# Four-stage cross attention on one core: where the norms' statistics stand, which engine takes the inverse root, and the listed order

## The chip, the cores and the metric

The kernel runs on one core of one Trainium2 chip, as one launch. The time is the device time in microseconds of that core. Lower is better. Engines: TensorE (PE in the profile, PEld its weight loads), VectorE (DVE), ScalarE (ACT), GpSimd (POOL) and SyncE (SP), which issues the DMAs.

## The reference

The input x is 16 batches of 128 rows by 256 columns in float32, ctx has the same shape. Four attention stages follow one another. In the excerpt below the names and masks are shortened.

```python
# stage 0: attention over the 256 columns of x, per batch, with ctx as keys and values
q, k, v = x^T Wq + bq, Wk^T ctx + bk, Wv^T ctx + bv
x = v softmax(q k)^T + x
# stage 1: 16 heads of 16; LN is (x - mean) * rsqrt(var + 1e-5) * scale + bias over the 256 columns
x = x + attention(LN1(x) @ w_qkv + b_qkv, causal mask) @ w_ao + b_ao
x = x + attention(LN2(x) @ w_q, ctx @ w_kv, cross mask) @ w_co + b_co
x = x + gelu(LN3(x) @ w1 + b1) @ w2 + b2
# stage 2: x are the latents; keys and values from ctx and x together
a = attention(x @ q_w, [ctx, x] @ kv_w, mask) @ out_w + out_b + x
x = gelu(RMS(a) * w @ mlp_w1 + b1) @ mlp_w2 + b2 + x
# stage 3: 16 heads of 128, one learned key and value more
x = x + attention(LNA(x) @ wq1, ctx @ wk1, ctx @ wv1) @ wo1 + bo1
x = x + attention(LNB(x) @ wq2, ctx @ wk2, ctx @ wv2) @ wo2 + bo2
x = x + gelu(LNM(x) @ w_fc1 + b_fc1) @ w_fc2 + b_fc2
```

There are thus four norms per batch in stages 1 and 2 (ln1, ln2, ln3 and rms) and three in stage 3.

## The kernel before

All of x lives in SBUF, in the tile X, for the whole kernel. Stages 0 to 2 are one block of code (`stages_0_to_2`), stage 3 is another (`stage_3`). In the block of stages 0 to 2 a group is two batches (NA = 2), so there are eight groups, 0 to 7. Work on several groups is interleaved. A name such as ln2/3 is norm ln2 of group 3. "chan" is stage 0's attention, "self" and "cross" are those of stage 1, "lat" that of stage 2, and mlp1 and mlp2 the two multilayer parts.

Each engine runs a list of pieces written out by hand: TENSOR_ORDER, VECTOR_ORDER, SCALAR_ORDER, GPSIMD_ORDER and LOAD_ORDER (for the DMA queue). A list is given as a string of letters, the *_STEPS, which says from which stream the next piece is taken. Engines work strictly in the order of their own list, and wait for each other through semaphores that are derived from the places in these lists.

A unit of attention goes through these pieces: "scores" (TensorE, L1118 and L1122, and L1110 for chan), "front" on VectorE (mask and row maximum, L801, L808, L779), "exps" (ScalarE, L640), "rsum" on VectorE (the reciprocal of the sum, L817), "normalise" on GpSimd (L590), "turn" on TensorE (transposition of the probabilities, L1135), a copy of it by ScalarE (L648) or VectorE (L823), and "values" on TensorE (L1155, L1165, L1168). After that come the output projection and the residual on VectorE (L839, or L828 for chan), which is followed by the statistics of its rows (bn_stats, L831 and L847).

A norm in stages 0 to 2 is one piece of VectorE. It waits for the xhat of the norm before, aggregates the statistics of the two batches (L859), adds epsilon (L867, for rms L863 and L865), makes the inverse root from an integer guess (L879, L881) and three Newton steps of three instructions each (L885, L887, L889), and then writes xhat (L873, L875). Each small instruction waits for the one before. TensorE transposes xhat (L984), ScalarE scales it on its way out of PSUM (L679, L681), and the projections read that. The statistics of ln1 lie in one buffer of two batches, `stats["ln1"]`, which every group's channel residual writes. A buffer with a place for each of the 16 batches, `row_stats`, holds the statistics of stage 2's result for stage 3's first norm.

GpSimd has, beside the normalises, the additions of bias rows to X (L571, L563), the masks (L577, L584) and, near the end, the low halves of split operands.

Stage 3 has two attention layers of eight pairs of heads. Their matmuls take operands split into a high and a low part, three passes each. GpSimd makes the low parts (L1522 for weights, L1532 for the normed rows, L1537 and L1543 for the last weights, L1549). A norm's factors come from `norm_factors` on VectorE for a slice of batches: aggregation (L1336), variance (L1338), guess (L1340, L1342), Newton steps (L1346, L1348, L1350) and the shift, minus mean times root (L1353). The even rows of xhat are then written by VectorE (L1855) and the odd ones by ScalarE (L1632), which waits for the shift. There are five calls: the first 12 batches while stages 0 to 2 run out, batches 12 to 15 at the opening of stage 3, all 16 at the turn between the two layers, and 0 to 7 and 8 to 15 at the end. At the end the last weights are split beside the norm.

Of the kernel before, what the change touches and what calls it, by code (L numbers as in the profile page):

```python
# [111 lines left out]
def steps_of(step, items):  # L112
# [14 lines left out]
    lat/0 self_q/2 self_k/2 cross_v/1 lat_k/0 lat_q/0 chan_v/3 self_v/2 ctx_v/0 chan_q/3 ctx_k/0 lat_v/0  # L127
    cross_k/2 chan_k/3 cross_o/1 self_o/2 ln3/1 mlp1_up1/1 ln2/2 mlp1_up0/1 cross_q/2 mlp1_up3/1 mlp1_up2/1
    mlp1_down0/1 mlp1_down1/1 ln1/3 lat/1 self_q/3 self_k/3 cross_v/2 lat_k/1 lat_q/1 lat_o/0 chan_v/4
    self_v/3 ctx_v/1 chan_q/4 ctx_k/1 lat_v/1 cross_k/3 chan_k/4 rms/0 cross_o/2 mlp2_up1/0 mlp2_up0/0  # L130
    mlp2_up2/0 mlp2_up3/0 self_o/3 ln3/2 mlp2_down0/0 mlp2_down1/0 mlp1_up1/2 ln2/3 mlp1_up0/2 cross_q/3
    mlp1_up3/2 mlp1_up2/2 mlp1_down0/2 mlp1_down1/2 ln1/4 lat/2 self_q/4 self_k/4 cross_v/3 lat_k/2 lat_q/2
    lat_o/1 chan_v/5 self_v/4 ctx_v/2 chan_q/5 ctx_k/2 lat_v/2 cross_k/4 chan_k/5 rms/1 cross_o/3 mlp2_up1/1
    mlp2_up0/1 mlp2_up2/1 mlp2_up3/1 self_o/4 ln3/3 mlp2_down0/1 mlp2_down1/1 mlp1_up1/3 ln2/4 mlp1_up0/3
    cross_q/4 mlp1_up3/3 mlp1_up2/3 mlp1_down0/3 mlp1_down1/3 ln1/5 lat/3 self_q/5 self_k/5 cross_v/4 lat_k/3
    lat_q/3 lat_o/2 chan_v/6 self_v/5 ctx_v/3 chan_q/6 ctx_k/3 lat_v/3 cross_k/5 chan_k/6 rms/2 cross_o/4
    mlp2_up1/2 mlp2_up0/2 mlp2_up2/2 mlp2_up3/2 self_o/5 ln3/4 mlp2_down0/2 mlp2_down1/2 mlp1_up1/4 ln2/5
# [122 lines left out]
def stages_0_to_2(nc, dram, consts, early):  # L260
# [8 lines left out]
    with ExitStack() as ctx:  # L269
# [207 lines left out]
        with nc.Block() as block:  # L477
# [280 lines left out]
            def _(dve):  # L758
# [90 lines left out]
                def norm(name, g):  # L849
# [1461 lines left out]
```

## Time and profile before

| | |
|---|---|
| runs | 2037.19, 2037.76, 2043.94 us; median 2037.76 |
| the profiled execution | 2035.49 us, its span 2033.5 |
| TensorE busy | 1916.0 us, 94% |
| VectorE busy | 1250.8 us, 62% |
| ScalarE busy | 1186.0 us, 58% |
| GpSimd busy | 676.1 us, 33% |
| stages 0 to 2 | up to about 880 us of the span |

The page's chain of waits puts half of the span on TensorE, most of it on stage 3's projections. Busy shares over the whole span hide the stages. From 100 to 880 us VectorE and ScalarE are busy around 80% beside TensorE; in stage 3 they are near half. The profile is of one execution, and times within it are counted from the start of its span.

### The profile page before, as it was taken

How to read it: one execution, taken by the hardware profiler on the slowest of the kernel's cores; microseconds unless marked ns; L12 is line 12 of the kernel's file. 1: busy time of each engine (PE TensorE's matmuls, PEld its weight loads, DVE VectorE, ACT ScalarE, POOL GpSimd, SP SyncE). 2: the span in 40 equal slices, each digit the busy share in tenths (PEclk: the TensorE clock that was granted, in tenths of full speed). 3: DMA queues.
4: the chain of work that ended last, by engine and by line, in shares of the span. 5: the costliest groups of instructions: out<-in, count | busy, mean ns of one | idle time of the engine just before them, and what ended most of it. 6: DMA issues, size and time to landing. Idle time of an engine off the chain costs nothing.

```text
span 2033.5 us, 43191 instructions
## 1 busy us (share of the span) xinstructions
PE 1916.0 (94%) x14880; PEld 1672.4 (82%) x14880; DVE 1250.8 (62%) x4143; ACT 1186.0 (58%) x3879; POOL 676.1 (33%) x613
## 2 busy tenths in 40 slices
PE   5689999999999999989999999999999999999888
PEld 3467878787878777778999999998899999999778
DVE  3678887887878774644555555556455555555753
ACT  3577888887888876654444444444544444444531
POOL 2334444444444434522221222232321222213452
PEclk7899999999999999999999999999999999999999
DMA  7000000000000000010000000000000000000100
GB/s 271 9 12 9 5 10 5 9 7 1 7 1 4 2 2 23 1 35 27 27 21 15 26 15 26 21 16 17 27 22 16 26 15 26 21 10 0 42 11 32
DMA packets 24635, 44.35 MB, mean 22 GB/s; under 512 B 2336, under 2 KB 12064, under 8 KB 23584
## 3 DMA queue, kind: packets, MB, share of 16 engines
q1 hardware_dynamic: 24336, 42.19, 6.4%
q8 instruction: 85, 1.39, 0.3%
q14 instruction: 70, 0.57, 0.1%
q10 hardware_dynamic: 144, 0.20, 0.0%
HBM read 40.28 MB, written 2.10 MB: 21 GB/s over the span
## 4 chain that ended last, share of the span: by engine, by line
PE 50%; DVE 2%; ACT 2%; issue 1%; POOL 1%; ACTq 0%; DVEq 0%; POOLq 0%
PE general L1988 33%; PE o_psum L2045 6%; PE scores L2027 5%; PE pT_psum L2104 3%; PE scores L2154 1%; ACT probs L1659 1%; POOL probs L1563 1%; PE o_psum L2154 1%; PE pT_psum L2154 1%; PE general L1999 0%; DVE oT L1830 0%; ACT oT L1675 0%; DVE guess L1340 0%; DVE var L1338 0%; DVE row_stats L1792 0%
## 5 line engine op out<-in xcount | busy, mean ns | idle before, releaser
L590 POOL TENSOR_TENSOR probs<-probs,rsums 128x512 f32<-128x512 f32 (+1 forms) x288 | 282.0, 994 | 429.6 <-DVE rsums L817 429.1
L1563 POOL TENSOR_TENSOR probs<-probs,rsums 128x512 f32<-128x512 f32 x128 | 133.3, 1041 | 733.1 <-DVE rsums L1823 733.1
L640 ACT ACTIVATE probs<-negated,negmax 128x128 f32<-128x128 f32 (+1 forms) x768 | 325.6, 429 | 32.8 <-DVE negmax L808 26.0
L1667 ACT COPY probsT<-pT_psum 128x512 f32<-128x512 f32 x128 | 75.0, 586 | 282.6 <-PE pT_psum L2104 282.6
L1988 PE MATMUL general<-hT,w_qk 128*128 128x512 f32 x768 | 206.3, 404 | 1.8 <-ACT kT L1642 1.5
L1135 PE MATMUL pT_psum<-ident,probs 128*128 128x128 f32 x1072 | 171.6, 280 | 33.7 <-ACT probsT L648 20.4
L1988 PE MATMUL general<-w_o,oT 128*128 128x256 f32 x1536 | 197.3, 281 | 1.6 <-ACT oT L1675 0.9
L1988 PE MATMUL general<-ctxT,w_qk 128*128 128x512 f32 x750 | 195.4, 396 | 2.9 <-DVEq L245 2.9
L1988 PEld LDWEIGHTS general<-w_o,oT 128*128 128x128 f32 x1536 | 187.4, 188 | 11.6 <-DVE oT L1830 4.0
L1675 ACT ACTIVATE oT<-o_psum,hcols 128x512 fp32r<-128x512 f32 x128 | 88.1, 689 | 183.8 <-PE o_psum L2045 183.8
L1659 ACT ACTIVATE probs<-scores,negmax 128x128 f32<-128x128 f32 x512 | 180.5, 370 | 24.0 <-DVE negmax L1815 24.0
L1135 PEld LDWEIGHTS pT_psum<-ident,probs 128*128 128x128 f32 x1072 | 123.7, 141 | 85.3 <-ACT probsT L648 38.4
L1988 PEld LDWEIGHTS general<-w_v,ctxT 128*128 128x128 f32 x1488 | 179.9, 189 | 4.6
L1988 PE MATMUL general<-w_v,ctxT 128*128 128x256 f32 x1488 | 181.9, 279 | 0.0
L1830 DVE SCALAR_TENSOR_TENSOR oT<-o_psum,hcols,oT 128x512 fp32r<-128x512 f32 x128 | 96.0, 750 | 119.5 <-ACT oT L1675 119.5
L1988 PEld LDWEIGHTS general<-ctxT,w_qk 128*128 128x128 f32 x750 | 140.1, 189 | 32.9 <-DVEq L245 3.3
L1988 PEld LDWEIGHTS general<-hT,w_qk 128*128 128x128 f32 x768 | 136.2, 189 | 26.5 <-issue 2.1
L997 PE MATMUL general<-hT_y,weights_a 128*128 128x256 f32 x640 | 152.1, 382 | 3.3 <-ACT upT L713 1.2
L640 ACT ACTIVATION_READ_ACCUMULATOR probs<-negated,negmax 128x1 f32 x768 | 147.3, 192 | 0.0
L2045 PE MATMUL o_psum<-probsT,ctxT 128*128 128x128 f32 x1024 | 141.5, 281 | 1.4 <-ACT probsT L1667 1.4
L823 DVE COPY probsT<-pT_psum 128x512 f32<-128x512 f32 (+1 forms) x140 | 91.2, 652 | 83.3 <-PE pT_psum L1135 82.1
L1812 DVE TENSOR_REDUCE rawmax<-scores 128x4 f32<-128x512 f32 x128 | 88.3, 690 | 83.8 <-PE scores L2027 83.8
(199 smaller groups left out, 3869.6 us busy)
## 6 DMA issues: line engine op xcount, KB each, us to landing
raw_qk<-w_qk_dram SPq DMA_DIRECT2D x32, 256.0 KB, 2.8
weights_a<-weights_a_dram SPq DMA_DIRECT2D x2, 2048.0 KB, 18.7
raw_v<-w_v_dram SPq DMA_DIRECT2D x16, 256.0 KB, 2.7
raw_vrows<-vrows_dram SPq DMA_DIRECT2D x16, 256.0 KB, 3.4
raw_o<-w_o_dram SPq DMA_DIRECT2D x16, 256.0 KB, 2.7
weights_a<-weights_a_dram SPq DMA_DIRECT2D x3, 1024.0 KB, 11.7
ctx_in<-ctx_dram SPq DMA_DIRECT2D x8, 256.0 KB, 2.9
X<-x_dram SPq DMA_DIRECT2D x8, 256.0 KB, 16.1
```

The lines of the kernel that those rows point to most:

```text
L590: nc.gpsimd.tensor_tensor(pr, pr, rsums[:, n % 4, 0:segs].unsqueeze(2).broadcast_to([P, segs, width(kind) // segs]), ALU.mult).then_inc(s[ ...
L640: last = nc.scalar.activation(probs[:, n % PROBS, i * wide:(i + 1) * wide], src[:, i * wide:(i + 1) * wide], ACT.Exp, scale=1.0 if kind == ...
L823: nc.vector.tensor_copy(probsT[:, n % 4, 0:width(kind)], turned(kind, g, u)[:, 0:width(kind)]).then_inc(s["pT_copied_dve"], 1)
L997: last = nc.tensor.matmul(out[:, j * RA:(j + 1) * RA], w[weight][:, c, chunk * P:(chunk + 1) * P], rhs(c), start=(c == 0), stop=(c == KC - 1))
L1135: last = nc.tensor.transpose(turned(kind, g, u)[:, j * P:(j + 1) * P], probs[:, n % PROBS, j * P:(j + 1) * P], ident[:, :])
L1563: nc.gpsimd.tensor_tensor(pr, pr, rsums[:, t % 2, :].unsqueeze(2).broadcast_to([P, NB, P]), ALU.mult).then_inc(s["probs_ready"], 1)
L1659: nc.scalar.activation(probs[:, t % 2, b * P:(b + 1) * P], scores[t % 2][:, b * P:(b + 1) * P], ACT.Exp, bias=negmax[:, t % 2, b:b + 1], s ...
L1812: nc.vector.tensor_reduce(rawmax[:, t % 2, :], scores[t % 2][:, :].rearrange("p (b k) -> p b k", b=NB), axis=AX.X, op=ALU.max, negate=True ...
L1830: nc.vector.scalar_tensor_tensor(out=oT[:, LO, head, quarter(t % G)], in0=o_psum[:, :], scalar=hcols[:, bass.ds(at, 1)], in1=oT[:, HI, hea ...
L1988: last = nc.tensor.matmul(out, stationary(a, c), moving(b, c), start=(i == 0), stop=(i == len(terms) - 1))
L2027: last = nc.tensor.matmul(scores[t % 2][:, j * P:(j + 1) * P], qT[:, head, b * P:(b + 1) * P], kT[:, head, b * P:(b + 1) * P], start=True, ...
L2045: last = nc.tensor.matmul(o_psum[:, j * P:(j + 1) * P], v[:, head, (t % G) * NB + j, :], probsT[:, j * P:(j + 1) * P], start=True, stop=True)
```

## The change

- The statistics of ln1 go into `row_stats`, at the place of each batch, in place of `stats["ln1"]`.
- The inverse root is one instruction of GpSimd: a power with exponent -0.5 from a constant tile `halves`, filled by a memset at the start. The guess and the Newton steps are gone, in stages 0 to 2 and in stage 3.
- A norm of stages 0 to 2 is now two pieces of VectorE, "norm" up to the variance and "xhat" behind it, with "root" on GpSimd between them. VectorE's list may have other pieces between the two. In stage 3 the five calls are split in the same way into `variances`, `inverse_roots` and `shifts`. The one for the first 12 batches is moved ahead in VectorE's list; its variance comes before the last group's units and its shift among them.
- The lists of all five queues are new. The strings differ in many places; the start of two of them is shown.

The lists, decoded: on GpSimd the two cross masks, which stood between the third and the fourth normalise of chan/0, stand behind the third normalise of self/0, and the mask of lat/0 moves from place 15 to place 5. On VectorE the pieces between norm and xhat number 0 in nine of the 32 norms, 1 in seven and up to 9 in the others. 408 lines of the decoded lists of TensorE differ between the two in a line by line comparison.

```diff
@@ -121,30 +121,30 @@
 WORK_ORDER = listed("""
-    chan_v/0 chan_q/0 chan_k/0 ln1/0 self_q/0 self_k/0 chan_v/1 self_v/0 chan_q/1 cross_k/0 chan_k/1 self_o/0
-    ln2/0 cross_q/0 ln1/1 self_q/1 self_k/1 cross_v/0 chan_v/2 self_v/1 chan_q/2 cross_k/1 chan_k/2 cross_o/0
+    chan_v/0 chan_q/0 chan_k/0 ln1/0 self_q/0 self_k/0 chan_v/1 chan_q/1 self_v/0 cross_k/0 chan_k/1 self_o/0
+    ln2/0 cross_q/0 ln1/1 self_q/1 chan_v/2 self_k/1 cross_v/0 self_v/1 chan_q/2 chan_k/2 cross_k/1 cross_o/0
...
 LOAD_WORDS = listed("""
-    ctx/2 ctx/3 mask_lat/1 mask_cross/2 ctx/4 mask_lat/2 mask_cross/3 ctx/5 mask_lat/3 mask_cross/4 ctx/6
-    mask_lat/4 mask_cross/5 ctx/7 mask_lat/5 mask_cross/6 mask_lat/6 mask_cross/7 mask_lat/7
+    mask_lat/1 ctx/2 mask_cross/2 ctx/3 mask_lat/2 ctx/4 mask_cross/3 mask_lat/3 ctx/5 mask_cross/4
+    mask_cross/5 ctx/6 mask_lat/4 mask_cross/6 mask_cross/7 mask_lat/5 ctx/7 mask_lat/6 mask_lat/7
...
 GPSIMD_STEPS = (
-    "pppxxpppppppappyppppappapppyppppxppppppppapp...
+    "ppppmyapppxxpyppppppmppmapappppppppppppppppm...
...
-                      w=steps_of("read", [...]), n=steps_of("norm", NORM_ORDER),
+                      w=steps_of("read", [...]), n=steps_of("norm", NORM_ORDER), q=steps_of("xhat", NORM_ORDER),
...
-                      k=..., z=[("first_norm", "x", GA - 1, 0)])
+                      k=..., z=[("first_norm", "x", GA - 1, 0)], i=[("first_shift", "x", GA - 1, 0)])
...
+GPSIMD_ORDER = merged(GPSIMD_STEPS, ..., m=steps_of("root", NORM_ORDER), ..., j=[("first_root", "x", GA - 1, 0)])
...
-        stats = {name: sb("stats_" + name, [P, NA, 6]) for name in NORMS}
+        stats = {name: sb("stats_" + name, [P, NA, 6]) for name in ("ln2", "ln3", "rms")}
...
+                nc.gpsimd.memset(consts["halves"][:, :], -0.5).then_inc(consts["halves_ready"], 1)
...
+                def root(name, g):
+                    pool.wait_ge(s["var_ready"], NORM_ORDER.index((name, g)) + 1)
+                    nc.gpsimd.tensor_tensor(rstd[:, :], var[:, :], consts["halves"][:, 0:NA], ALU.pow).then_inc(s["root_ready"], 1)
...
-                    step(nc.vector.bn_stats(stats["ln1"][:, b, :], x))
+                    step(nc.vector.bn_stats(consts["row_stats"][:, NA * g + b, :], x))
...
-                        step(nc.vector.bn_aggr(mv[:, b, :], stats[name][:, b, :]))
+                        step(nc.vector.bn_aggr(mv[:, b, :], consts["row_stats"][:, NA * g + b, :] if name == "ln1" else stats[name][:, b, :]))
...
-                        step(nc.vector.tensor_scalar(var[:, :], mv[:, :, 1], 1e-5, None, ALU.add))
-                    wait_step()
-                    inverse_root()
+                        nc.vector.tensor_scalar(var[:, :], mv[:, :, 1], 1e-5, None, ALU.add).then_inc(s["var_ready"], 1)
+
+                def xhat_of_rows(name, g):
+
+                    src = Xl[:, :, :] if name == "rms" else X[:, batches(g), :]
+                    dve.wait_ge(s["root_ready"], NORM_ORDER.index((name, g)) + 1)
+                    dve.sem_inc(s["wait_passed"], 1)
...
-                def inverse_root():
-                    step(nc.vector.tensor_single_scalar(guess[:, :], var[:, :].bitcast(I32), 1, ALU.logical_shift_right))
-                    wait_step()
-                    step(nc.vector.tensor_scalar(guess[:, :], guess[:, :], -1.0, RSQRT_MAGIC, ALU.mult, ALU.add))
-                    wait_step()
-                    y = guess[:, :].bitcast(F32)
-                    for i in range(NEWTON_STEPS):
...
+def variances(dve, early, stats, bs):
+    nc = early["nc"]
+    mv, var = early["mv"], early["var"]
+    for b in range(bs.start, bs.stop):
+        early["steps"][0] += 1
+        nc.vector.bn_aggr(mv[:, b, :], stats[:, b, :]).then_inc(early["s"]["norm_step"], 1)
+    dve.wait_ge(early["s"]["norm_step"], early["steps"][0])
+    nc.vector.tensor_scalar(var[:, bs], mv[:, bs, 1], 1e-5, None, ALU.add).then_inc(early["s"]["factors_var"], 1)
+
+def inverse_roots(pool, early, consts, bs, call):
+    pool.wait_ge(early["s"]["factors_var"], call)
+    early["nc"].gpsimd.tensor_tensor(early["rstd"][:, bs], early["var"][:, bs], consts["halves"][:, bs], ALU.pow).then_inc(early["s"]["factors_root"], 1)
+
+def shifts(dve, early, bs, call):
+    dve.wait_ge(early["s"]["factors_root"], call)
+    early["nc"].vector.scalar_tensor_tensor(out=early["shift"][:, bs], in0=early["mv"][:, bs, 0], scalar=-1.0, in1=early["rstd"][:, bs],
+                                            op0=ALU.mult, op1=ALU.mult).then_inc(early["s"]["norm_ready"], 1)
...
                         if kind == "end":
+                            if t == STEPS - 1:
+                                inverse_roots(pool, early, consts, slice(0, B // 2), 4)
...
                     if kind == "turn":
+                        inverse_roots(pool, early, consts, slice(0, B), 3)
                         for g in range(G):
                             split_h(a + 1, g)
 
+                inverse_roots(pool, early, consts, slice(FIRST_BATCHES, B), 2)
                 for g in range(G):
                     split_h(0, g)
...
                 split_h(2, 0)
                 split_h(2, 1)
+                inverse_roots(pool, early, consts, slice(B // 2, B), 5)
                 for half in range(2):
                     down_weights_low(half)
```

## Rows read from the trace of the kernel before

**Rows 1.** The page's first line.
```profile
span 2033.5 us, 43191 instructions
```

**Rows 2.** Busy time by stretch: stretch, length, PE, PEld, DVE, ACT, POOL, clock, DMA.
```profile
0.00:100.00 100.00, 60.43 (x412) 44.29 (x412) 53.14 (x242) 42.05 (x158) 25.96 (x34) 0.85 0.39 142
100.00:200.00 100.00, 87.41 (x822) 68.66 (x820) 79.77 (x371) 77.94 (x295) 39.54 (x41) 1.00 0.03 8
200.00:700.00 500.00, 483.94 (x4470) 400.47 (x4474) 407.08 (x1859) 419.48 (x1395) 221.49 (x221) 1.00 0.02 6
700.00:880.00 180.00, 167.97 (x1414) 136.76 (x1404) 103.96 (x447) 116.88 (x345) 75.68 (x67) 1.00 0.02 8
880.00:900.00 20.00, 16.48 (x105) 14.30 (x106) 13.50 (x32) 11.98 (x18) 5.80 (x3) 0.91 0.26 86
1390.00:1412.00 22.00, 19.20 (x153) 18.04 (x152) 17.73 (x60) 7.32 (x19) 1.04 (x1) 0.96 0.00 1
1908.00:1948.00 40.00, 29.10 (x153) 24.44 (x153) 33.19 (x81) 22.88 (x40) 20.54 (x12) 0.87 0.00 1
```

**Rows 3.** Groups by line on DVE, 0 to 880: busy, mean ns, idle before.
```profile
L887 DVE TENSOR_TENSOR newton<-newton,var 128x2 f32<-128x2 f32 x96 | 15.4, 161 | 3.3
...
L885 DVE SCALAR_TENSOR_TENSOR newton<-guess 128x2 f32<-128x2 f32 x32 | 5.1, 160 | 1.1
```

**Rows 4.** Waits of PE, 0 to 130: total, times, longest.
```profile
PE general L984 <- DVE xhat_x L875: 13.4, 3, 5.3
```

**Rows 5.** Timeline of the start: start, length, instruction, idle before it and releaser.
```profile
16.34 0.15 DVE L817 RECIPROCAL rsums<-sums 128x1 f32<-128x1 f32 x1
...
18.29 0.89 POOL L577 TENSOR_SCALAR madd_cross<-mask_cross 128x256 f32<-128x256 f32 x2 [2.22 <-DMA mask_cross<-mask_cross_dram]
...
19.26 0.61 POOL L590 TENSOR_TENSOR probs<-probs,rsums 128x256 f32<-128x256 f32 x1
...
20.02 0.66 PE L1135 MATMUL pT_psum<-ident,probs 128*128 128x128 f32 x2 [1.94 <-POOL probs L590]
...
24.69 0.17 DVE L867 TENSOR_SCALAR var<-mv 128x2 f32<-128x2 f32 x1
...
27.06 0.73 DVE L875 TENSOR_SCALAR xhat_x<-X,mv,rstd 128x256 f32<-128x256 f32 x2
...
27.85 1.11 PE L984 MATMUL general<-ident,xhat_x 128*128 128x128 f32 x4 [4.57 <-DVE xhat_x L875]
```

**Rows 6.** Timeline at the opening of stage 3.
```profile
890.22 4.84 POOL L1532 TENSOR_TENSOR hT<-kT,hT 128x1024 fp32r<-128x1024 f32 x2 [39.69 <-ACT hT L1646]
890.41 2.25 DVE L1353 SCALAR_TENSOR_TENSOR shift<-mv,rstd 128x4 f32<-128x4 f32 x1
...
896.20 0.66 PE L1999 MATMUL general<-ident,xhat 128*128 128x128 f32 x4 [1.80 <-DVE ctxT L1805]
```

**Rows 7.** Timeline at the turn of stage 3, PE.
```profile
1408.72 3.01 PE L1999 MATMUL general<-ident,qT 128*128 128x128 f32 x16 [2.08 <-DVE ctxT L1805]
```

**Rows 8.** Groups by line on POOL, whole span.
```profile
L552 POOL TENSOR_SCALAR madd_self<-mask_self 128x128 f32<-128x128 f32 x1 | 0.3, 298 | 4.0 <-DMA mask_self<-mask_self_dram 4.0
```

**Rows 9.** Waits of PE, 200 to 700.
```profile
PE pT_psum L1135 <- DVE probsT L823: 3.9, 8, 0.8
```

**Rows 10.** Timeline at the end of stage 3's second layer.
```profile
1912.33 2.36 POOL L1537 TENSOR_TENSOR ctxT<-ctxT 128x1024 fp32r<-128x1024 f32 x1
1912.44 2.28 DVE L1340 TENSOR_SCALAR guess<-var 128x8 int32<-128x8 int32 x1
...
1918.28 3.50 PE L1999 MATMUL general<-ident,qT 128*128 128x128 f32 x16 [3.26 <-DVE qT L1855]
...
1927.08 4.76 POOL L1543 TENSOR_TENSOR ctxT<-kT,ctxT 128x1024 fp32r<-128x1024 f32 x2
1927.09 2.42 DVE L1338 TENSOR_SCALAR var<-mv 128x8 f32<-128x8 f32 x1
...
1936.90 5.49 PE L1988 MATMUL general<-hT,ctxT 128*128 128x512 f32 x12 [4.00 <-ACT qT L1706]
```

More of the change, by code:

```diff
@@ L128 @@
     cross_k/2 chan_k/3 cross_o/1 self_o/2 ln3/1 mlp1_up1/1 ln2/2 mlp1_up0/1 cross_q/2 mlp1_up3/1 mlp1_up2/1
[L129 to L137, printed above, removed]
+    mlp1_down0/1 mlp1_down1/1 ln1/3 lat/1 self_q/3 cross_v/2 self_k/3 lat_k/1 lat_q/1 lat_o/0 chan_v/4 ctx_v/1
@@ new lines @@
+    self_v/3 chan_q/4 ctx_k/1 lat_v/1 cross_k/3 chan_k/4 rms/0 cross_o/2 mlp2_up1/0 mlp2_up0/0 mlp2_up3/0
+    mlp2_up2/0 self_o/3 ln3/2 mlp2_down0/0 mlp2_down1/0 mlp1_up1/2 ln2/3 mlp1_up0/2 cross_q/3 mlp1_up3/2
+    mlp1_up2/2 mlp1_down0/2 mlp1_down1/2 ln1/4 lat/2 self_q/4 cross_v/3 self_k/4 lat_k/2 lat_q/2 lat_o/1
+    chan_v/5 chan_q/5 ctx_v/2 self_v/4 ctx_k/2 cross_k/4 lat_v/2 chan_k/5 rms/1 cross_o/3 mlp2_up1/1
+    mlp2_up3/1 mlp2_up2/1 mlp2_up0/1 self_o/4 ln3/3 mlp2_down0/1 mlp2_down1/1 mlp1_up1/3 ln2/4 mlp1_up0/3
@@ L138 @@
+    cross_q/4 mlp1_up2/3 mlp1_up3/3 mlp1_down0/3 mlp1_down1/3 ln1/5 lat/3 self_q/5 self_k/5 cross_v/4 lat_k/3
+    lat_q/3 lat_o/2 chan_v/6 self_v/5 ctx_v/3 chan_q/6 lat_v/3 ctx_k/3 cross_k/5 chan_k/6 rms/2 cross_o/4
+    mlp2_up1/2 mlp2_up0/2 mlp2_up2/2 mlp2_up3/2 self_o/5 ln3/4 mlp2_down0/2 mlp2_down1/2 ln2/5 mlp1_up1/4
     mlp1_up0/4 cross_q/5 mlp1_up3/4 mlp1_up2/4 mlp1_down0/4 mlp1_down1/4 ln1/6 lat/4 self_q/6 self_k/6
-    cross_v/5 lat_k/4 lat_q/4 lat_o/3 chan_v/7 self_v/6 ctx_v/4 chan_q/7 ctx_k/4 lat_v/4 cross_k/6 chan_k/7
@@ new lines @@
+    mlp2_up0/4 mlp2_up1/4 mlp2_up2/4 mlp2_up3/4 self_o/7 ln3/6 mlp2_down0/4 mlp2_down1/4 mlp1_up1/6 ln2/7
+    mlp1_up0/6 cross_q/7 mlp1_up2/6 mlp1_up3/6 mlp1_down0/6 mlp1_down1/6 lat/6 cross_v/7 lat_k/6 lat_q/6
+    lat_o/5 ctx_v/6 ctx_k/6 lat_v/6 rms/5 cross_o/7 mlp2_up3/5 mlp2_up1/5 mlp2_up2/5 mlp2_up0/5 ln3/7
+    mlp2_down0/5 mlp2_down1/5 mlp1_up3/7 mlp1_up0/7 mlp1_up1/7 mlp1_up2/7 mlp1_down0/7 mlp1_down1/7 lat/7
+    lat_k/7 lat_q/7 ctx_v/7 lat_o/6 ctx_k/7 lat_v/7 rms/6 mlp2_up1/6 mlp2_up3/6 mlp2_up0/6 mlp2_up2/6
@@ L611, in _ @@
                         normalise(kind, g, u)
+                    elif piece == "root":
+                        root(kind, g)
+                    elif piece == "first_root":
+                        inverse_roots(pool, early, consts, slice(0, FIRST_BATCHES), 1)
                     elif piece == "first_low":
@@ L957, in _ @@
                         chan_residual(g, u // 2)
+                    elif piece == "first_shift":
+                        shifts(dve, early, slice(0, FIRST_BATCHES), 1)
                     elif piece == "norm":
                         norm(kind, g)
+                    elif piece == "xhat":
+                        xhat_of_rows(kind, g)
                     else:
@@ L1849, in norm_factors_of @@
                     dve.sem_inc(s["wait_passed"], 1)
-                    norm_factors(dve, early, stats, bs)
+                    variances(dve, early, stats, bs)
+                    shifts(dve, early, bs, call)
                 def xhat_rows(g):
```

137 lines of the change are left out of this document (51 added, 86 removed).

## The prediction

> **What bounds the kernel now.** I read the page first, then the busy times by stretch, then the waits of TensorE in the stretches where it is idle, and last the order of time around each of these. The profiled execution took 2035.49 us, of which the span is 2033.5 [rows 1]; it lies 2.3 us below the median of the three runs, 2037.76. The table by stretch is what decides [rows 2]: the reader is to subtract each PE entry from the length of its stretch. From 200 to 700 us, the steady part of stages 0 to 2, TensorE is idle for 16.1 of 500 us, at the full clock. In the first 100 us it is idle for 39.6 and the granted clock is 0.85; from 100 to 200 for 12.6; while stage 2 runs out (700 to 880) for 12.0. The three places in stage 3 where a norm stands between attention layers cost 3.5 (880 to 900), 2.8 (1390 to 1412) and 10.9 (1908 to 1948). VectorE is busy 81% from 200 to 700 and does the norms, but it is not the bound there. So the change can win in the idle stretches and little in between.
>
> **The buffer for the row statistics.** Before, ln1's statistics were one pair of columns, so a batch's channel residual of the next group had to come after ln1 of the group before. In the new vector order, as in the old, both channel residuals of every group 1 to 7 stand behind ln1 of the group before by dozens of pieces (group 2: places 107 and 112, ln1/1 at 51). The freedom isn't used by this order. It changes no instruction's size: 0 us, and nothing hides it.
>
> **What VectorE loses.** For each of the 32 norms of stages 0 to 2, eleven small instructions go (two for the guess, nine Newton steps), 352 in seven groups of the answer by lines, of which the first and the last stand in [rows 3]. The seven sum to 58.8 us busy and 12 us idle ahead of them: 2.2 us a norm, 71 us in all, one after another, since each waits for the one before. In stage 3 the same eleven go from each of five calls at about 0.2 us each, 2.3 us a call. What comes instead is a power on GpSimd and two hand-overs, and VectorE's wait for it.
>
> **The root's price.** No row shows a power. From below: GpSimd's smallest arithmetic on real data, 128x128, took 0.30 us [rows 8]. From above: its longest instructions here took 2.4 us each, for 1024 columns (two in 4.84) [rows 6]; that the function itself is slower still I keep as a rival. Two columns are nearer to the 0.30 row, and I take 0.3 us, 0.5 for the 8 to 16 columns of stage 3. A hand-over between engines cost 0.06 us where TensorE took up xhat: 27.06 + 0.73 to 27.85 [rows 5]; I take 0.1 for each of the two. So from variance to root known is 0.17 + 0.1 + 0.3 + 0.1 = 0.7 us where it was 27.06 - 24.69 = 2.4 [rows 5]. Saved where exposed: 1.6 us. The 32 roots put 10 us on GpSimd, which is busy 44% from 200 to 700 [rows 2].
> The Trainium skill's page "GPSIMD Engine Reference", section "Performance versus the Vector engine", says that GpSimd's dispatch passes two software steps and that it is about half as fast on elements. Only that page has such a price for the unseen operation, and its factor on VectorE's 0.16 us would make the root 0.3 as well, without telling what the power function adds.
>
> **The start (0 to 200 us).** Three waits for xhat_x cost TensorE 13.4 us [rows 4]: ln1/0, ln2/0 and ln1/1. Each chain loses 1.6: 4.9 us. The fourth exposed norm, ln2/1 at 138 us, loses another 1.6, taken from the same difference. Then the order. GpSimd had the two cross masks ahead of the fourth normalise; that reciprocal was done at 16.49, the masks waited for their load until 18.29 and the normalise began at 19.26 [rows 5]. The new order has them behind the third normalise of self/0. TensorE waited 1.94 for it before its transpose at 20.02: 1.9 us. Around ln2/0 three transposes and one value product of chan/1 now stand between self_o/0 and the norm, where before two score products did; I give this and the front put between norm and xhat of ln1/1 2.5 us. Sum 10.9; parts of these waits will turn into waits for whatever comes next, so I take 9.
> The load list: a mask now goes ahead of ctx/2 on SP's queue, and its wait is for the mask of group 0 on GpSimd, moved from place 15 to 5. Behind it on GpSimd stand the bias of self/0 and the first normalise of self/0, which needs two projections, scores and exponentials after ln1/0; that covers the load. Cost 0, at most 1 if the load came late.
>
> **The middle and the running out (200 to 880).** 2.2 us a norm is 8% of VectorE's time, but only 3.9 of TensorE's 16.1 us idle are waits for VectorE's copies [rows 9]; most wait for ScalarE's. I take 3 us for 200 to 700 and 1.5 of the 12.0 behind it.
>
> **Stage 3.** Opening: the shift (L1353) took 2.25 us because GpSimd's subtraction of h had begun 0.2 earlier, and TensorE then waited 1.80 for VectorE's copy behind it [rows 6]. With 2.3 - 0.7 us less ahead of it the shift comes at about 888.8, before the subtraction at 890.22, which waits for ScalarE: the 1.8 go. Turn: TensorE waited 2.08 behind the same chain of 16 columns [rows 7]: 2.3 - 1.0 = 1.3 go. End: at 1912.44 an instruction of 0.17 took 2.28 beside GpSimd's subtraction of weights, and TensorE waited 3.26 for xhat at 1918.28 [rows 10]. GpSimd does the root before that subtraction now, so the shift is what stands beside it: 1912.7 + 2.4 + 0.2 = 1915.3 instead of 1914.7 and eleven more at 0.2 = 1916.9, 1.6 us. At 1927.09 one of 0.17 took 2.42 and the next was held as long, so the shift came at 1927.1 + 4.8 + 2.2 = 1934.1, and TensorE waited 4.00 at 1936.90 for ScalarE, whose work stands behind that shift. Now variance and root come before GpSimd's pair of subtractions (4.76 us), and the shift is held through the first only: 1927.8 + 2.4 = 1930.2. The 3.9 are not all TensorE's: the pair itself starts 0.7 later and GpSimd's next work with it, so I take 2.5. Stage 3 together: 1.8 + 1.3 + 1.6 + 2.5 = 7.2.
> The rows show small VectorE instructions with SBUF inputs ending when GpSimd's ends [rows 6, 10]. The Trainium skill's "SBUF — State Buffer", section "Who interferes with whom", makes this a rule: a VectorE instruction with two SBUF inputs is held for the whole of a GpSimd instruction that reads SBUF. It speaks against the change at the end, where the shift (two SBUF inputs) follows the root directly and GpSimd goes straight on; by it the first end saves 1.6, without it 3.3 and the sum would be 1.7 larger.
>
> **Sum.** 9 + 3 + 1.5 + 7.2 = 20.7. Against it: in nine of the 32 norms no piece stands between norm and xhat in the new vector order, so VectorE stands for some 0.5 us each, and every listed order has seams that I can't see; I take 4 us for both. 2035.5 - 16.7 = 2018.8 on the profiled execution's scale; plus 2.3 for the median: 2021 us. Its own range is 2010 to 2029.
>
> **Rivals.**
> Only stage 3 gains: the start's waits move to ScalarE's and VectorE's softmax work; then 2037.8 - 7.2, about 2030. For it: of the 39.6 us idle in the first 100 [rows 2], 26 are not waits for xhat and so stand on those engines. Against: nothing else has single waits of 5 us there [rows 4].
> No change: the gains of stage 3 are lost in new seams of the tensor order, whose two versions differ in 408 lines, or the root costs the 2.2 it replaces: 2036. Against: its stages' idle is plain.
> Slower, by the root: the power is a long software function. At 3 us for two columns and 0.75 a column beyond, the four exposed norms lose (3.4 - 2.2) x 4 = 5, the turn 13 - 2, the opening 4, the two ends (7 - 2) x 2 = 10, and 32 x 3 us in GpSimd's queue hold up normalises, some 0.3 each, 10; less the 1.9 for the mask and what else the order gives, 15 at most: 2058. It decides from about 2 us for two columns upward. For it: nothing in the trace excludes it. Against: the new order puts one or no piece between norm and xhat for half of the norms, which would leave VectorE standing long.
> Slower, by the queue: GpSimd works in order, and a root waits for the variance while normalises behind it may be ready. In the new lists the next normalise's reciprocal stands ahead of the norm in five cases of 32; if these and late residuals cost TensorE 0.5 us a norm, 16 us, less 7 from stage 3: 2047.
>
> **Chances.** Forecast 0.58, only stage 3 0.12, no change 0.14, slow root 0.10, queue 0.06. About 0.3%, 6 us, is what can be told from no change. Faster 0.70, same 0.14, slower 0.16. The range from 2008 to 2044 leaves out the slow root, most of the queue's tail and a little of a larger gain: 2 in 10.
>
> **What would show it.** The power's rows on GpSimd: near 0.3 us, below 1. VectorE's 407 us from 200 to 700 down to about 370. TensorE's wait for xhat_x in the first 130 us from 13.4 to 6 or less; its idle time in the first 200 us from 52 to about 43. The shift at the opening at 0.17 us, at the ends still stretched above 2. The waits of 3.26 and 4.00 us at the ends below 2. It is wrong if the power takes over 2 us, if TensorE's idle from 200 to 700 grows above 20 us, or if idle in the first 200 stays at 50.

## The result, and the profile after

The changed kernel took 2005.86, 2006.49 and 2011.93 us, median 2006.49, against 2037.76: the ratio is 0.9848, with a 95% interval of 0.9817 to 0.9879. The direction was the predicted one and the size was not: 31.3 us against a forecast of 16.7, just outside the stated range from 2008 to 2044. The profiled execution took 2006.49 us, with 2004.5 in the span.

The stretches of [rows 2] are cut here at the same work in both traces: at the norm ln1/2, at ln1/5 and at stage 3's first matmul. The first fence is the kernel before, the second the changed one (columns as in [rows 2]).

```profile
0.00:156.63 156.63, 106.82 (x838) 80.95 (x839) 96.08 (x441) 84.39 (x308) 45.28 (x54) 0.90 0.26 95
156.63:431.07 274.44, 264.43 (x2436) 216.36 (x2436) 224.08 (x1023) 232.55 (x775) 121.40 (x122) 1.00 0.03 7
431.07:881.04 449.97, 428.49 (x3835) 352.90 (x3834) 323.80 (x1453) 339.95 (x1111) 195.99 (x185) 1.00 0.02 6
881.04:2033.50 1152.46, 1116.30 (x7774) 1022.22 (x7774) 606.88 (x1227) 529.15 (x1689) 313.42 (x252) 0.99 0.07 22
```

```profile
0.00:143.02 143.02, 103.22 (x834) 79.14 (x835) 88.09 (x375) 80.44 (x298) 51.20 (x62) 0.93 0.30 104
143.02:409.96 266.94, 262.10 (x2437) 216.39 (x2436) 207.54 (x905) 237.68 (x781) 127.95 (x132) 1.00 0.02 6
409.96:852.77 442.81, 426.02 (x3839) 353.15 (x3838) 301.25 (x1277) 337.63 (x1114) 209.24 (x201) 1.00 0.02 6
852.77:2004.50 1151.73, 1115.19 (x7774) 1022.20 (x7774) 592.41 (x1183) 529.00 (x1689) 322.35 (x256) 0.99 0.07 22
```

Read the second column: the stretches lost 13.6, 7.5, 7.2 and 0.7 us. So 28.3 of the 29.0 us lie in stages 0 to 2, more than half of it behind the start, and stage 3 gave almost nothing. From 200 to 700 us TensorE's idle time fell from 16.1 to 7.1 us. Of the 14.7 us lost behind ln1/2, 9.9 are idle time of TensorE and 4.8 are busy time for the same products; what shortened the latter isn't shown.

The waits of TensorE for the copies of the turned probabilities, from 200 us to the end of stage 2, before and after (us in total, times, longest; the second line of each answers to [rows 9]):

```profile
PE pT_psum L1135 <- ACT probsT L648: 11.4, 20, 0.8
PE pT_psum L1135 <- DVE probsT L823: 4.7, 9, 0.8
```

```profile
PE pT_psum L1138 <- ACT probsT L659: 4.4, 9, 0.7
PE pT_psum L1138 <- DVE probsT L834: 3.1, 6, 0.8
```

The waits that I had put out of VectorE's reach, because they are for ScalarE, are the ones that fell most. The two lines together account for 8.6 of the 14.7 us. At the start the wait of [rows 4], 13.4 us in three, fell to this (0 to 200 us, and the same up to 130):

```profile
PE general L987 <- DVE xhat_x L889: 6.1, 2, 3.3
```

The root itself, by shape, in the changed kernel (busy us, mean ns, idle before):

```profile
L612 POOL TENSOR_TENSOR rstd<-var,halves 128x2 f32<-128x2 f32 x32 | 22.7, 709 | 72.8 <-DVE var L877 60.8 <-DVE var L875 11.7
...
L1339 POOL TENSOR_TENSOR rstd<-var,halves 128x8 f32<-128x8 f32 x2 | 3.3, 1643 | 0.4 <-DVE var L1332 0.3
L1339 POOL TENSOR_TENSOR rstd<-var,halves 128x16 f32<-128x16 f32 x1 | 2.9, 2913 | 11.2 <-DVE var L1332 11.2
```

It is 0.71 us for two columns, where I took 0.3, and 1.64 and 2.91 for 8 and 16, where I took 0.5. The gain is larger than forecast although the root is dearer.

### The profile page after: what moved, and what is told of

Same layout as the page of the kernel before. It is cut to its first block, busy times and chain, and to the rows that moved or that the text cites. A ratio compares the mean times of both kernels' runs of the same rounds, so it can differ in the third digit from the quotient of the medians.

```text
span 2004.5 us, 42854 instructions
## 1 busy us (share of the span) xinstructions
PE 1906.5 (95%) x14880; PEld 1670.9 (83%) x14880; DVE 1189.3 (59%) x3736; ACT 1184.8 (59%) x3879; POOL 710.7 (35%) x651
## 4 chain that ended last, share of the span: by engine, by line
PE 51%; ACT 2%; DVE 2%; issue 2%; POOL 1%; ACTq 0%; DVEq 0%; POOLq 0%
PE general L1988 34%; PE o_psum L2045 6%; PE scores L2027 5%; PE pT_psum L2104 3%; PE scores L2154 1%; ACT probs L1658 1%; PE o_psum L2154 1%; PE pT_psum L2154 1%; ACT oT L1674 1%; DVE oT L1829 1%; POOL probs L1557 1%; PE general L1999 0%; POOL rstd L1339 0%; ACT kT L1641 0%; DVE shift L1346 0%
## 5 line engine op out<-in xcount | busy, mean ns | idle before, releaser
L651 ACT ACTIVATE probs<-negated,negmax 128x128 f32<-128x128 f32 (+1 forms) x768 | 325.6, 431 | 15.5 <-DVE negmax L819 11.5
```

Source lines behind the costliest of these rows:

```text
L651: last = nc.scalar.activation(probs[:, n % PROBS, i * wide:(i + 1) * wide], src[:, i * wide:(i + 1) * wide], ACT.Exp, scale=1.0 if kind == ...
```

## The experiments

Each was timed beside the kernel before. "New" and "old" are the listed orders; the ratios are to the kernel before on the same chip. The rows come from several chips, so ratios are compared across rows, and medians only roughly.

| label | what it is | median us | ratio, 95% |
|---|---|---|---|
| h0 | all roots by power, old order | 2034.8 | 0.9979 (0.9964 to 0.9995) |
| e2 | power in stages 0 to 2 alone, old order | 2038.3 | 0.9991 (0.9976 to 1.0005) |
| e9 | no root at all in stages 0 to 2, old order | 2032.0 | 0.9965 (0.9952 to 0.9979) |
| e11 | h0, and the 11 instructions as load | 2070.1 | 1.0165 (1.0141 to 1.0188) |
| e1 | new order, Newton steps in stages 0 to 2 | 2054.5 | 1.0072 (1.0051 to 1.0094) |
| e10 | changed kernel, 5 instructions as load | 2033.4 | 0.9977 (0.9962 to 0.9993) |
| e5 | changed kernel, 11 instructions as load | 2069.0 | 1.0144 (1.0123 to 1.0165) |
| e6 | changed kernel, three powers for one | 2026.4 | 0.9947 (0.9929 to 0.9966) |
| h2, 24 | power, new order behind ln1/7 | 2024.0 | 0.9942 (0.9925 to 0.9960) |
| h2, 16 | power, new order behind ln1/5 | 2025.1 | 0.9938 (0.9920 to 0.9956) |
| h2, 8 | power, new order behind ln1/3 | 2019.0 | 0.9900 (0.9878 to 0.9922) |
| h2, 5 | power, new order behind ln1/2 | 2018.0 | 0.9894 (0.9871 to 0.9916) |
| e4 | changed kernel, pair buffer for ln1 | 2006.7 | 0.9854 (0.9834 to 0.9873) |
| e7 | kernel before, cross masks moved | 2037.9 | 0.9994 (0.9978 to 1.0011) |
| e3 | kernel before, stage 3 by power | 2035.7 | 0.9989 (0.9975 to 1.0003) |
| e8 | changed kernel, row copies ahead | 2001.3 | 0.9824 (0.9808 to 0.9840) |
| e12 | e8, the turn by Newton steps | 2003.1 | 0.9829 (0.9807 to 0.9851) |

**Order or root.** First each half alone.

```diff
 # e1, on the changed kernel: in norm(), behind the variance
+                    wait_step()
+                    inverse_root()
 # e2, on the kernel before: in norm()
-                    inverse_root()
+                    dve.wait_ge(s["root_ready"], NORM_ORDER.index((name, g)) + 1)
```

> The changed kernel with all its new lists and its stage 3, but with the inverse root of the 32 norms of stages 0 to 2 back on VectorE as guess and three Newton steps (in the norm piece; GpSimd's root pieces are dropped). Theory A, the listed order pays for most of the 28 us of stages 0 to 2: only the four exposed chains get longer, by about 1.3 us each (2.4 against the 1.1 that variance to root takes with a power of 0.71 us), so 2006.5 + 5 to 8, about 2012 to 2015. Theory B, the new lists only collect what the relieved VectorE gives (71 us less of it): most of the gain is lost, 2025 or more. Theory C, both count about half: 2017 to 2022.

> The kernel before with its old lists and its old stage 3, but with the root of the 32 norms of stages 0 to 2 as a power on GpSimd: VectorE stands between variance and xhat, and the roots are put into GpSimd's old list behind the last normalise whose reciprocal stands ahead of the norm. Theory A (the order pays): the four exposed chains save 1.3 us each, 2037.8 - 5 = 2033, at most 2030. Theory B (VectorE's load pays, whatever the order): 2020 or less. Theory C: 2024 to 2029.

No theory held in both. e1 lies in the open range of theory B, and far beyond it: the new order with Newton steps is slower than the kernel before, by 0.7%. e2 excludes theory B: the power in the old order gives nothing that is clear of noise, less even than theory A had. Both together give 1.5%. h0 completes the square: all of the code's change, old order.

> The changed kernel's code (ln1's statistics per batch, all roots by power, stage 3 as changed) with the old listed order of all five queues; xhat stands directly behind its norm in VectorE's list, the roots where the old lists' power kernel had them. Theory O (the gain exists only where new order and short norm meet): 2033 to 2038, since the root alone gave 0.9991 and stage 3 alone 0.9989 of the time. Rival: code and order add up, and the new lists with Newton steps were slow only because GpSimd's additions stood in front of the probabilities; then this one is below 2025.

It came out as theory O has it. The old order has xhat directly behind its norm, so VectorE stands for the root. The waits of VectorE for it in the changed kernel, and in h0:

```profile
DVE xhat_x L889 <- POOL rstd L612: 4.8, 7, 0.9
DVE xhat_y L889 <- POOL rstd L612: 4.7, 4, 1.8
DVE xhat_y L887 <- POOL rstd L612: 2.3, 3, 0.9
```

```profile
DVE xhat_x L888 <- POOL rstd L611: 15.3, 16, 1.3
DVE xhat_y L888 <- POOL rstd L611: 8.3, 8, 1.8
DVE xhat_y L886 <- POOL rstd L611: 7.6, 8, 1.0
```

31.2 us in 32 waits against 11.8 in 14: the pieces between norm and xhat hide 19 us of standing. That alone isn't why h0 gains so little, as e9 shows, in which nobody waits for a root.

```diff
 # e9, on the kernel before: the root is left out, xhat takes the variance
-                    inverse_root()
...
-  nc.vector.tensor_scalar(xhat[:, b, :], src[:, b, :], mv[:, b, 0:1], rstd[:, b:b + 1], ...)
+  nc.vector.tensor_scalar(xhat[:, b, :], src[:, b, :], mv[:, b, 0:1], var[:, b:b + 1], ...)
```

> The kernel before with its old lists, and in stages 0 to 2 no inverse root at all: guess and Newton steps are left out, xhat multiplies by the variance instead of the root, so the output isn't the reference's. VectorE loses 71 us and waits for nobody. If VectorE's standing for the power (23 us in 24 waits) hid the gain in the kernel with old lists and power: 2020 or less. If TensorE's and ScalarE's old order is the bound from 200 to 880 us and only the exposed chains count: 4 x 2.4 = 8 to 10 us at most, 2028 to 2034, with TensorE's busy time from 200 to 700 within 1 us of 484.

71 us less on VectorE are worth 7 us in the old order (0.35%), about what the exposed chains give: TensorE's waits for xhat_x in the first 200 us fell from 15.0 to 6.0 us. TensorE's busy time from 200 to 700 us was 485.4, 1.4 from the 484 of [rows 2], where within 1 had been expected; the changed kernel has 492.9. So VectorE's time isn't the bound in the old order, and what is left are the places of TensorE's and ScalarE's pieces; e9 doesn't tell which.

**What VectorE's time is worth in either order.** The old instructions come back as load, behind xhat.

```diff
 # e5, on the changed kernel; e11 the same on h0; e10 with one Newton step in place of three
                         ins.then_inc(s["xhat_ready"], 1)
+                    wait_step()
+                    load_only()      # guess and Newton steps into a tile that nothing reads
```

> The changed kernel, where VectorE makes the same eleven guess and Newton instructions after the xhat of each of the 32 norms of stages 0 to 2, into a tile that nothing reads: the chain to xhat is as short as in the changed kernel, but VectorE's load of 71 us is back. If the shorter chain is what the removed instructions were worth: 2006.5 to 2009. If it is VectorE's time, because everything behind the norm in VectorE's list comes 2.2 us earlier: the same time as the new lists with Newton steps in the chain, within 3 us.

> The changed kernel with five of the eleven old instructions (guess and one Newton step, about 1.0 us a norm, 32 us in all) made by VectorE behind xhat, into a tile that nothing reads. If VectorE's time is the price, in proportion to the eleven (62 us for 71): 2006.5 + 28 = 2034. If the new order has slack up to some load: below 2020.

> The changed kernel's code with the old lists, and all eleven instructions made by VectorE behind xhat. If the old order is indifferent to VectorE's time (it gained 0.2% when it was freed): 2035 to 2040, against 2034.8 without this load. If VectorE's time has one price in any order: 2095.

In the new order 71 us cost 62 and 32 us cost 27: 0.87 and 0.84 us for each. The chain to xhat was short in both, so it is VectorE's time that this order needs, and already at 32 us there is no slack for it. e5 missed one expectation: it was to come within 3 us of e1 and is 14.5 us slower. Both do the eleven instructions, but VectorE in e5 also stands 12.2 us for roots; e1 against the changed kernel has 71 us more work and 11.8 less standing, 59 in all, for 48 us, 0.8 again.

Both expectations of e11 fell. The old order isn't indifferent, and the price isn't the same either: against h0 the 71 us cost 35, half. Against the kernel before, e11 has the same instructions and 31 us of standing more, and is 33 us slower. A kink where the order was fitted fits both: a microsecond more on VectorE costs about one, a microsecond less gives a tenth (e9), and 40 at a tenth with 31 at one make 35. TensorE's waits in e5, 200 to 914 us, show where load goes: to copies and residuals behind the norm, and to probabilities of GpSimd.

```profile
PE o_psum L1189 <- DVE probsT L835: 10.9, 7, 4.2
PE pT_psum L1156 <- POOL probs L592: 10.6, 8, 3.1
PE pT_psum L1156 <- DVE probsT L835: 8.4, 12, 1.7
PE general L1005 <- DVE X L851: 7.7, 5, 2.5
PE pT_psum L1156 <- ACT probsT L660: 6.2, 12, 0.8
```

The same in e1, 200 to 900 us, where GpSimd has no roots in these stages:

```profile
PE o_psum L1186 <- DVE probsT L834: 7.4, 5, 3.8
PE pT_psum L1153 <- POOL probs L591: 6.7, 7, 1.6
PE pT_psum L1153 <- DVE probsT L834: 6.6, 10, 1.8
```

The changed kernel has 0.7, 0.6 and 3.1 us of these three. So the wait for probabilities comes without roots on GpSimd too. Late reciprocals of VectorE can make it, and so can GpSimd's queue, in which additions stand for xhat (in e1 58.7 us in ten waits) and roots for variances; the two weren't separated. The waits for ScalarE's copies, on the other hand, go with the order and not with VectorE's load. From 200 us to the end of stage 2 they are 4.4, 4.8, 5.3, 5.3 and 6.2 us in the changed kernel, e6, e1, e10 and e5, and 9.6, 10.4, 11.1 and 11.4 in h0, e9, e11 and the kernel before. e11's line:

```profile
PE pT_psum L1155 <- ACT probsT L659: 11.1, 19, 0.8
```

```diff
 # e6, on the changed kernel, in root()
+                    for i in range(2):
+                        nc.gpsimd.tensor_tensor(spare[:, at:at + NA], var[:, :], consts["halves"][:, 0:NA], ALU.pow)
```

> The changed kernel with two more powers on GpSimd ahead of each root of stages 0 to 2, into a tile that nothing reads: the chain from variance to xhat is 1.4 us longer, VectorE has no more work. If only the four exposed chains count: 2006.5 + 6 = 2012. If VectorE's standing at xhat counts as its work does (9 of 32 norms have no piece in between, 7 one): 20 norms x 1.4 x 0.87 = 24, so 2030. 45 us more on GpSimd cost nothing in either case if its queue has room.

20 us (24 by the expectation). VectorE stood 36.7 us for the root instead of 11.8, 25 more: 0.8 a microsecond again, as if standing cost what work costs. TensorE's waits for GpSimd's probabilities also rose, from 0.6 to 3.8 us, so a part of the 20 may be GpSimd's longer queue; this wasn't separated. It also tests my rival of the slow root, which was to decide from about 2 us: with 2.1 us in the chain two thirds of the gain are gone (11 of 31 us are left), and the change is still faster.

**Where in the order.** The h2 kernels have the power and follow the old order up to a norm, the new one behind it. There is no code change but the strings.

> The changed kernel, whose lists follow the old order up to the norm ln1/2 (about 156 us) and the new order behind it; all roots by power. By the ledger of the two traces (13.6 us of the 28.3 of stages 0 to 2 are gained up to ln1/2, of which the root alone gives 0.7 to 1.5): 2006.5 + 12 = 2018 to 2020. By my prediction's terms (9 us for the start, 3 for the middle): 2014 to 2016. If the new order pays as a whole only, because the seam costs: 2028 or more.

> As the last, with the old order up to ln1/3 (about 234 us). By the ledger (17.2 us up to there): 2006.5 + 16 = 2022 to 2024. If all of the start's gain lies ahead of ln1/2: the same as the last within 1 us.

> The changed kernel with the old listed order up to ln1/5 (about 431 us of the kernel before) and the new one behind it. Old order to ln1/2 gave 2018.0, to ln1/3 2019.0, throughout 2034.8. By the ledger of the two traces 3.9 us lie between ln1/3 and ln1/5 and 7.4 behind: 2019 + 4 = 2023. If the late part (the last groups, and the running out with the first norm of stage 3) holds most of what is left: 2020 or less. If each group gives the same (16 us over five groups): 2025.

> As the last, with the old order up to ln1/7 (about 628 us) and the order of the loads as before. By the ledger: 2023 to 2025, with 7 to 9 us of the gain behind ln1/7, where my prediction gave 1.5. If each group gives the same: 2031. If it is 2033 or more, the running out gives nothing, as my term had it.

From h0 downwards: the new order behind ln1/7 gives 0.37%, from ln1/5 on no more than that, from ln1/3 on 0.79% in all, from ln1/2 on 0.85%, and the start the last 0.46%. In us of 2037 that is 17.3 behind ln1/2 and 9.4 for the start (16.8 and 11.5 by the medians). Of the four steps from h0 to h2, 5, two are smaller than their intervals, and the intervals on both sides of ln1/3 to ln1/5 and of the start just overlap. So three parts are told apart, the last alone clearly: the start, the groups between ln1/3 and ln1/5, and what lies behind ln1/7. The sums by trace came out for ln1/2 and ln1/7; for ln1/3 they gave 2022 to 2024 where 2019 was measured, so they place the gain of single groups only roughly.

**The single terms.**

```diff
 # e4, on the changed kernel
-  step(nc.vector.bn_stats(consts["row_stats"][:, NA * g + b, :], x))
+  step(nc.vector.bn_stats(stats["ln1"][:, b, :], x))
 # e7, on the kernel before
-    "pppxxpppppppappy...
+    "pppppppxxpppappy...
```

> The changed kernel with the statistics of ln1 in one pair of columns again, as before. My prediction: the order doesn't use the freedom, 0 us, 2006.5 within 2. Rival: the checked order of writes and reads costs VectorE waits somewhere: 2010 or more.

> The kernel before with the two cross masks moved behind the third normalise of self/0 on GpSimd's list, nothing else. My prediction's term: TensorE's wait of 1.94 us ahead of its fourth transposition (at 20.0 us) goes, all of the start comes 1.9 us earlier, 2035.3; ln1/0's xhat is transposed at 25.9 instead of 27.85. Rival: the gain is there at 26 us and given back by the waits for masked scores and copies ahead of ln2/0, whose xhat then stands at 71.2 as before.

The buffer is worth nothing, as predicted. The masks gain 1.6 us at ln1/0 (26.26 against 27.85 of [rows 5]) and nothing at ln2/0, 71.12 against 71.17 before:

```profile
26.26 1.11 PE L984 MATMUL general<-ident,xhat_x 128*128 128x128 f32 x4 [4.58 <-DVE xhat_x L875]
...
71.12 1.01 PE L984 MATMUL general<-ident,xhat_x 128*128 128x128 f32 x4 [3.48 <-DVE xhat_x L875]
```

The rival's figures held, but not its reason. The waits ahead of ln2/0 took nothing back: at 54.32 us e7 was still 1.4 us ahead (55.69 before). The same 36 products behind that were made at the lower level of TensorE's clock, where the kernel before had the higher one. The stretches of these products, e7 and then before, columns as in [rows 2]:

```profile
54.30:57.60 3.30, 2.95 (x36) 2.09 (x36) 0.21 (x2) 0.55 (x3) 3.25 (x4) 0.50 0.00 0
```

```profile
55.70:57.60 1.90, 1.63 (x36) 1.19 (x36) 0.18 (x2) 0.47 (x3) 1.88 (x2) 1.00 0.00 0
```

At ln1/1 e7 is even 1.0 us behind (87.36 against 86.34), again after slower products. So in this execution the masks' gain went to the clock. Over ten runs the time is that of the kernel before as well, but whether the clock takes it each time isn't shown.

> The kernel before with only four of stage 3's five norm calls changed (opening, turn, both ends: power on GpSimd at the changed kernel's places); stages 0 to 2 as before. My prediction's term: 7.2 us, so 2030.5. Read from the changed kernel's trace, where stage 3 lasts 1151.7 us instead of 1152.5: 0.7 us, so 2037, and TensorE idle of over 5 us in front of the third quarter's products of the multilayer part, where the second end's gain is given back.

The interval (0.9975 to 1.0003) excludes 7.2 us; its stage 3 lasts 1152.2 us in the profile, 0.3 less than before. Its edit is stage 3's part of the change but for the first call.

**A better kernel.** The second end in the changed kernel, VectorE, GpSimd and TensorE in turn (start, length, instruction, idle before it):

```profile
1900.53 2.35 DVE L1346 SCALAR_TENSOR_TENSOR shift<-mv,rstd 128x8 f32<-128x8 f32 x1 [1.75 <-POOL rstd L1339]
...
1908.37 1.66 DVE L1955 TENSOR_TENSOR oT<-qT,oT 128x512 fp32r<-128x512 f32 x1
1909.96 1.49 DVE L1952 CAST oT<-qT 128x512 fp32r<-128x512 f32 x1
...
1916.10 1.52 DVE L1863 TENSOR_SCALAR kT<-general,cols 128x512 f32<-128x512 f32 x2
...
1906.74 8.89 POOL L1543 TENSOR_TENSOR oT<-qT,oT 128x512 fp32r<-128x512 f32 x5 [1.53 <-DVE oT L1952]
...
1905.71 3.04 PE L1988 MATMUL general<-hT,ctxT 128*128 128x512 f32 x12 [1.29 <-ACT qT L1705]
1908.59 1.91 PE L1999 MATMUL general<-ident,xhat 128*128 128x128 f32 x16
1916.99 2.90 PE L1988 MATMUL general<-hT,ctxT 128*128 128x512 f32 x6 [6.49 <-issue]
```

TensorE's 4.00 us of [rows 10] are 1.29, so the norm does come earlier. Then TensorE is idle for 6.49 us (2.03 before), because the copy L1863 stands behind casts and subtractions of VectorE that are stretched beside GpSimd's five (1.49 us a cast, where six in a row just ahead took 2.09), and which now begin earlier too.

```diff
-                up_parts(0)
+                up_parts(0, range(FC - LATE))
                 norm_copy("end", 2, 2)
                 norm_copy("end", 2, 3)
+                up_parts(0, range(FC - LATE, FC))
```

> The changed kernel, where VectorE copies the normed rows of quarters 2 and 3 of the last norm (L1863) ahead of its last three high parts of the first quarter (L1952, L1955), not behind them. In the changed kernel's trace these six instructions are stretched beside GpSimd's subtractions, 7.9 us from 1908.4 to 1916.1, and TensorE is idle for 6.49 us behind them. If this queue is where the second end's gain was given back, the idle falls to about 2.5: 2006.5 - 4 = 2002.5. If GpSimd's own subtractions (8.9 us for five), which stand ahead of the splits of quarters 2 and 3 on its queue, set the end of that wait: 2006 to 2007.

2001.3 us, 0.24% under the changed kernel's ratio. These two intervals overlap, but e4, which is the changed kernel but for the buffer, was timed on the same chip: four runs from 2005.8 to 2009.6 us against five from 2000.7 to 2003.2. The idle time is gone altogether. The rows of e8:

```profile
1910.34 1.69 DVE L1863 TENSOR_SCALAR kT<-general,cols 128x512 f32<-128x512 f32 x2 [1.32 <-issue]
...
1909.60 1.91 PE L2000 MATMUL general<-ident,xhat 128*128 128x128 f32 x16
1911.27 1.63 PE L1989 MATMUL general<-hT,ctxT 128*128 128x512 f32 x6
```

e8 beats both kernels: 36 us under the one before.

```diff
 # e12, on e8, at the turn
-                        inverse_roots(pool, early, consts, slice(0, B), 3)
...
+                    norm_factors(dve, early, stats, bs)      # guess, Newton steps and shift, as before
```

> The changed kernel with the row copies ahead (as e8, which gave 2001.3), and at the turn of stage 3 the old guess and Newton steps on VectorE in place of the power over 16 columns. The power took 2.91 us and two hand-overs, the eleven small instructions 2.2: TensorE's wait at the turn (2.77 us in the changed kernel, 2.08 before) goes back to 2.1, and the time is the same as that of e8 within 1 us, 2000.5.

TensorE's wait at the turn is 2.08 us, as before the change, and 2.76 in e8: the power over 16 columns, in place of the eleven instructions, is the cause. The time can't tell the two apart: 2003.1 us, where 2000.5 within 1 was expected, with intervals that overlap. The rows, e8's and e12's:

```profile
1381.29 2.45 PE L2000 MATMUL general<-ident,qT 128*128 128x128 f32 x16 [2.76 <-DVE ctxT L1804]
```

```profile
1392.06 2.45 PE L2037 MATMUL general<-ident,qT 128*128 128x128 f32 x16 [2.08 <-DVE ctxT L1838]
```

## Why the prediction was right in direction and wrong in size

**The step that failed: "the middle and the running out".** I gave 3 and 1.5 us for 200 to 880, from the row that only 3.9 of 16.1 us idle are waits for VectorE [rows 9], and so priced the lighter VectorE in the order of before. In that order the price was about right: e9 gives 7 us over all of stages 0 to 2, and h0 4 with stage 3. But the order is a term of its own. Behind ln1/2 it measured 17 us (h0 against h2, 5), of which 7.5 behind ln1/7, with the short norm as its condition: without it the new order costs 0.7% (e1). The order takes away the waits for ScalarE's copies, whatever VectorE does (4.4 to 6.2 us against 9.6 to 11.4). Behind ln1/2 the new list of TensorE has 10 pairs of transpositions with nothing between them, the old one 17; that this is the reason is argued, not shown. With the short norm VectorE's copies and GpSimd's probabilities come in time too; with the long one TensorE waits 16 us more for them (e1). I had seen that 408 lines of TensorE's list differ and allowed seams against it, 4 us, where the lists with the short norm carried most of the gain.

**The start, 9 us.** By the traces 13.6 up to ln1/2; by the runs 9 to 12 for the order there, and little for the root alone. The size is near, the parts are not: the masks' 1.9 come to nothing by ln2/0 (e7), and the chains' 1.6 (2.4 less 0.7 is 1.7) are about 1.3 with a root of 0.71. In e2 the three waits for xhat_x of [rows 4] fell by 4.4 us in sum, and the total did not move: the granted clock was 0.78 in the first 100 us (0.85 before), where TensorE made some pieces from 57 to 74 us at the lower of its two levels, and 0.97 from 800 to 850 (1.00 before). The clock of the first 100 us lies between 0.76 and 0.86 in the profiles of kernels with the old start and between 0.78 and 0.93 in those with the new one. It changes from execution to execution: e3, which up to stage 3 is the kernel before, had 0.81 for its 0.85. So a part of the 13.6 us, read from one trace each, may be clock (0.90 against 0.85), and my terms had none. Why it fell in e2 stays open.

**Stage 3, 7.2 us.** Measured 0.7 in the trace, 2.2 (up to 5.1) in e3. The opening's wait of 1.80 is gone as predicted, and the root took 1.01 us. That put TensorE 2.2 us ahead. Then 1.6 of it were lost to the clock: behind a wait that the kernel before has as well, the products of the changed kernel are slow (granted clock 0.64 from 876.3 to 881.0, 1.00 at the same work before).

```profile
876.39 0.95 PE L2104 MATMUL pT_psum<-ident,probs 128*128 128x128 f32 x4 [2.47 <-POOL probs L1557]
877.13 1.92 PE L2027 MATMUL scores<-kT,qT 128*128 128x128 f32 x8
```

(before: 0.66 and 1.06, behind the same idle 2.47). The turn lost 0.7 instead of gaining 1.3, since I had the root at 0.5 and it is 2.91. The first end gained 0.4 of 1.6, for the same reason (1.64). The second end gained 2.7 at the wait that I had read, 2.5 forecast, and gave 4.5 back in the queue behind it; I had said that GpSimd's next work starts later with the pair and had not followed VectorE's queue to L1863. The clock moved twice beside this: the twelve products behind the shorter wait took 3.04 us for 5.49 [rows 10], and the six behind the longer one 2.90 for this row's 1.62 before.

```profile
1946.34 1.62 PE L1988 MATMUL general<-hT,ctxT 128*128 128x512 f32 x6 [2.03 <-issue]
```

Counted from stage 3's first matmul, the changed kernel is 0.8 us late behind these seams. What makes its stage 3 0.7 us shorter after all comes at the very end, behind an equal wait, before and after:

```profile
2017.25 7.47 PE L2154 MATMUL scores<-ctxT,oT 128*128 128x256 f32 x48 [1.77 <-DVE X L1965]
```

```profile
1989.77 5.98 PE L2154 MATMUL scores<-ctxT,oT 128*128 128x256 f32 x48 [1.77 <-DVE X L1965]
```

So by this pair of traces the norms of stage 3 gave nothing, and the 0.7 is clock.

**What held.** The buffer at 0. TensorE's idle time in the first 200 us, 43.0 (about 43 forecast, 52 before), though its parts were others. VectorE's busy time from 200 to 700, 375.8 (about 370 forecast). The power under 1 us for two columns, and no harm from GpSimd's queue: it stood 73 us for variances, and TensorE's waits for its probabilities from 200 us on were 0.6 us in sum, 0.8 before. The shifts at the ends took 2.32 and 2.35 us beside GpSimd's subtractions, and the one at the opening, with nothing beside it, 0.17. The Trainium skill's page "SBUF — State Buffer", section "Who interferes with whom", says that a VectorE instruction with two SBUF inputs contends with a GpSimd instruction that reads SBUF. The trace agrees for the shift, whose inputs are mv and rstd. L1340 and L1338 of [rows 10] have one input and were held too, at 2.28 and 2.42 us, which the rule on two inputs doesn't cover. The waits at the ends were to be below 2 us: they were 2.81 and 1.29.

## What to carry to other kernels

When a hand-written order and an operation's cost change together, price them as one: build the square of old and new in both before believing either. In this kernel's two orders, time added to VectorE, 75 to 81% busy from 200 to 700 us, cost about 0.8 to 1 of its length, and time taken from it gave a tenth until the order was made again. When a wait goes, follow every queue behind it to the next instruction that another engine needs.

## What was not expected of the hardware

The power on GpSimd is 0.71, 1.01, 1.64, 2.27 and 2.91 us for 2, 4, 8, 12 and 16 columns: (2.91 - 0.71) / 14 = 0.157 us a column on 0.4. VectorE's small instructions are 0.17 us for 2 as for 16, with some 0.03 between two, so by estimate eleven of them (2.2 us) are cheaper than the power with its two hand-overs (0.1 in all) from about 11 columns.

The spread of the kernel before goes with its clock: eight runs with a mean granted clock of 0.980 took 2043.7 to 2047.1 us, 37 with 0.987 took 2034.7 to 2039.8. In its profile, a run at 0.987, the loss lies in the first 100 us and at the seams of stage 3; no run at 0.980 was profiled. Between kernels the clock differs too: the median run had 0.987 in the kernel before, 0.990 in the changed one, 0.983 in e1, e5 and e11, and 0.984 in e2. From about 8 us for 0.007, the estimate is 3 to 4 us of the changed kernel's 31, and some 5 us of what e1, e5 and e11 lose against the kernel before. No main reading changes by it.
